# An attention kernel whose POOL engine takes over a quarter of the low parts, with value products carried over units

## The reference

```
x = x + tanh(g_xattn[i]) * attention_i(...)
x = x + tanh(g_ffn[i]) * experts_i(...)
```

```
dots = jnp.einsum('bhid,bhjd->bhij', q, k) * scale
attn = jax.nn.softmax(dots, axis=-1)
out = jnp.einsum('bhij,bhjd->bhid', attn, v)
return out @ Wo + bo
```

## Time and profile before

| | |
|---|---|
| median of 3 runs | 3818.83 us (3818.24 to 3830.18) |
| the profiled execution, its own time | 3806.05 us |
| its span, first to last instruction | 3804.4 us |
| PE busy | 3136.1 us (82%) |
| DVE busy | 1952.9 us (51%) |
| ACT busy | 1442.8 us (38%) |
| POOL busy | 698.3 us (18%) |
| granted clock of PE, mean | 0.864 of full speed |

### The profile page before, as it was taken

The page is one execution under the profiler, slowest core; times in us unless marked ns, Lnnn a source line. Parts: engine busy times, 40 slices in busy tenths (PEclk is TensorE's granted clock), DMA queues, the critical chain, the costliest instruction groups (busy, mean ns, idle before and its releaser), DMA issues. The chain is left out here.

```text
span 3804.4 us, 47742 instructions
## 1 busy us (share of the span) xinstructions
PE 3136.1 (82%) x13932; PEld 2131.8 (56%) x13933; DVE 1952.9 (51%) x3544; ACT 1442.8 (38%) x2976; POOL 698.3 (18%) x808
## 2 busy tenths in 40 slices
PE   7594769982898798999499999999999998349990
PEld 4493434432885477999356556555565664226650
DVE  3313454412453315444578777787777885613333
ACT  1131443430211113444346666666666666001100
POOL 0101021113103110000211112211112211061116
PEclk6697769995997568999689999999999999679995
DMA  1442000005232001000000000000000000324543
GB/s 34 151 146 70 1 1 1 1 1 197 87 103 62 13 0 45 23 22 1 9 6 2 8 1 7 5 4 6 2 7 1 7 1 3 136 99 152 167 141 109
DMA packets 136512, 174.12 MB, mean 46 GB/s; under 512 B 36345, under 2 KB 112784, under 8 KB 132784
## 3 DMA queue, kind: packets, MB, share of 16 engines
q1 hardware_dynamic: 104992, 103.23, 8.3%
q0 software_dynamic: 17072, 47.34, 3.8%
q10 hardware_dynamic: 14304, 22.02, 1.7%
HBM read 110.20 MB, written 62.00 MB: 45 GB/s over the span
## 5 line engine op out<-in xcount | busy, mean ns | idle before, releaser
L1853 DVE TENSOR_TENSOR l3a_pt_lo<-l3a_pt,l3a_pt_hi 128x512 fp32r<-128x512 f32 (+1 forms) x640 | 467.6, 733 | 161.3 <-ACT l3a_pt L1749 157.6
L1748 ACT ACTIVATE l3a_pt_hi<-l3a_banks 128x512 fp32r<-128x512 f32 (+1 forms) x640 | 381.8, 597 | 368.1 <-PE l3a_banks L1709 305.0
L1749 ACT ACTIVATE l3a_pt<-l3a_banks 128x512 f32<-128x512 f32 (+1 forms) x640 | 378.1, 591 | 0.0
L1828 DVE TENSOR_REDUCE l3a_maxima<-l3a_banks 128x1 f32<-128x1178 f32 x256 | 353.0, 1382 | 23.2 <-PE l3a_banks L1662 14.1
L1719 PE MATMUL l3a_banks<-l3a_q,l3a_k 128*128 128x512 f32 (+1 forms) x640 | 278.0, 434 | 26.2 <-ACT l3a_pt L1749 24.7
L1709 PE MATMUL l3a_banks<-l3a_pt_hi,l3a_v 128*65 128x512 f32 (+1 forms) x640 | 287.9, 450 | 2.0 <-ACT l3a_out L1762 1.6
L1720 PE MATMUL l3a_banks<-l3a_q,l3a_k 72*128 72x512 f32 (+3 forms) x640 | 256.9, 401 | 0.0
L1709 PE MATMUL l3a_banks<-l3a_pt_lo,l3a_v 128*65 128x512 f32 (+1 forms) x640 | 253.6, 396 | 0.0
L1709 PE MATMUL l3a_banks<-l3a_pt_hi,l3a_v_lo 128*65 128x512 f32 (+1 forms) x640 | 253.2, 396 | 0.0
L1662 PE MATMUL l3a_banks<-l3a_k,l3a_q 64*128 64x512 f32 (+1 forms) x768 | 210.8, 382 | 5.3 <-DVE l3a_maxima L1828 4.1
L1719 PEld LDWEIGHTS l3a_banks<-l3a_q,l3a_k 128*128 128x128 f32 (+1 forms) x640 | 117.3, 183 | 120.2 <-issue 37.8
(11 more groups left out here) (525 smaller groups left out, 6273.0 us busy)
## 6 DMA issues: line engine op xcount, KB each, us to landing
l3f_w<-in_L_ffn_w SPq DMA_DIRECT2D x96, 256.0 KB, 3.0
l0f_w<-in_L_ffn_W ACTq DMA_DIRECT2D x12, 1024.0 KB, 6.5
l3f_slots_x<-l3f_zeros SPq DMA_DIRECT2D x10, 1024.0 KB, 12.7
l1f_w<-in_L_ffn_W ACTq DMA_DIRECT2D x18, 512.0 KB, 4.6
l2f_w<-in_L_ffn_w SPq DMA_DIRECT2D x16, 512.0 KB, 4.3
l3f_x_rows<-l3f_slots_x SPq DMA_DIRECT2D x32, 256.0 KB, 4.1
l3f_slots_y<-l3f_y_rows POOLq DMA_DIRECT2D x32, 256.0 KB, 4.0
l1f_slots_x<-l1f_zeros SPq DMA_DIRECT2D x5, 1024.0 KB, 8.1
```

Of the source, the lines that this page charges most:

```text
L1748: act.activation(a.pt_hi[0:rows, n % a.pt_slots, :], a.st_bank[0:rows, n % 2, :], ACT.Exp, bias=bias, scale=scale)
L1749: act.activation(a.pt[0:rows, n % 4, :], a.st_bank[0:rows, n % 2, :], ACT.Exp, bias=bias, scale=scale).then_inc(a.exped, 1)
L1828: dve.tensor_reduce(a.maxima[:, n:n + 1], banks.rearrange("p a b -> p (a b)")[:, 0:KEYS], AX.X, ALU.max).then_inc(a.maxed, 1)
L1853: dve.tensor_tensor(a.pt_lo[0:rows, slot, :], a.pt[0:rows, n % 4, :], a.pt_hi[0:rows, slot, :].bitcast(F32), ALU.subtract).then_inc(a.lo_m ...
```

## The change

- Low parts: of every four slots of layer 3, the low part of the fourth (n = 3, 7, ..., 39) is made by POOL, in order with its other work; DVE makes the other three. PE and ACT wait for the one or the other engine's count (`low_of`). `pt_hi` and `pt_lo` have 5 buffers and not 6.
- POOL's program of a unit: before slot 14 it scales group 3 of the unit before, before slots 20, 30 and 39 groups 0, 1 and 2, and between them it makes the low parts in order of slots.
- The copies of q and k are DMAs on SP's queue, ahead of the totals of group 3 of the unit before; DVE inverts these totals in slot 12 and not in slot 4.
- The value products of a unit's last 4 (2) slots come in the first slots of the next unit, and so does the keeping of its group 3.
- The scores for the maxima are matmuls over 128 rows (rounded q twice against rounded k and the rest of k), and so wait for the copies of q and for all of k.
- In the last unit, four tiles of its own output projection run in slots 36 to 39, and four after it.
- The first unit stands before the loop: in layer 3 the loop has 6 rounds, 3 units follow it.

```
-        self.pt_slots = 6 if split else 4
+        self.pt_slots = 5 if split else 4
...
 def scores_pe(...)
+        project.keys_ready(pe, 0 if unit is None else unit, uses)
+        pe.wait_ge(a.q_doubled, 64 if unit is None else unit * 64 + 64)
-    lhs = a.q1[hi, u, h, t * P:(t + 1) * P]
+    lhs = a.q1[:, u, h, t * P:(t + 1) * P]
...
-        ins = pe.matmul(banks[:, c, 0:end - at], lhs, a.k1[hi, u, h, at:end], start=True, stop=not masked)
+        ins = pe.matmul(banks[:, c, 0:end - at], lhs, a.k1[:, u, h, at:end], start=True, stop=not masked)
...
 def attention_pe(...)
         if n >= a.lag:
-            multiply_values(n - a.lag)
-    for n in range(SLOTS_OF_UNIT - a.lag, SLOTS_OF_UNIT):
-        multiply_values(n)
+            multiply_values(unit, u, n - a.lag)
+        elif not is_first(unit):
+            multiply_values(unit - 1, 1 - u, SLOTS_OF_UNIT + n - a.lag)
...
 def attention_act(...)
+        if n == a.lag and not is_first(unit):
+            keep_group(act, a, unit - 1, GROUPS - 1)
...
-            act.wait_ge(a.lo_made, unit * SLOTS_OF_UNIT + (n + 1))
+            if not (is_first(unit) and n < a.exp_slots):
+                act.wait_ge(*low_of(a, unit, n - a.exp_slots))
...
 def attention_dve(...)
-        if a.split:
+        if a.split and not low_by_pool(a, n):
...
-def attention_pool(pool, a, unit, u, following=True):
-    scale_group(pool, a, number(unit, -1), 3, 1 - u)
+def attention_pool(pool, a, unit, u):
+    scaled_at = {14: -1, 20: 0, 30: 1, 39: 2}
+    for n in range(SLOTS_OF_UNIT):
+        if n in scaled_at:
+            g = scaled_at[n]
+            if a.split:
+                pool.wait_ge(a.lo_made_pool, unit * (SLOTS_OF_UNIT // 4) + n // 4)
+                pool.sem_inc(a.passed, 1)
+            scale_group(pool, a, number(unit, g), g % GROUPS, 1 - u if g < 0 else u)
+            pool.wait_ge(a.ot_done, number(unit, g) + 3)
+            pool.sem_inc(a.passed, 1)
+        if low_by_pool(a, n):
+            slot, rows = n % a.pt_slots, key_chunk(n % 10)[1]
+            pool.wait_ge(a.exped, unit * SLOTS_OF_UNIT + (n + 1 + 2))
+            pool.sem_inc(a.passed, 1)
+            pool.tensor_tensor(a.pt_lo[0:rows, slot, :], a.pt[0:rows, n % 4, :], a.pt_hi[0:rows, slot, :].bitcast(F32),
+                               ALU.subtract).then_inc(a.lo_made_pool, 1)
...
+def low_by_pool(a, n):
+    return a.split and n % 4 == 3
...
+def low_of(a, unit, n):
+    if low_by_pool(a, n):
+        return a.lo_made_pool, unit * (SLOTS_OF_UNIT // 4) + (n + 1) // 4
+    return a.lo_made, unit * (SLOTS_OF_UNIT // 4 * 3) + (n + 1 - (n + 1) // 4)
...
-def double_parts(pool, a, unit, u):
+def double_parts(sp, a, unit, u):
...
-                out, source = a.q1[other, u, h, columns], a.q1[hi, u, h, columns]
+                sp.dma_start(a.q1[other, u, h, columns].bitcast(F32), a.q1[hi, u, h, columns].bitcast(F32)).then_inc(a.q_doubled, 16)
```

More of the change, by code:

```diff
@@ L1615, in attention_prepare, with is_first @@
     pool.tensor_scalar(a.minus[:], chip.ident[0:8, 0:8], -1.0, None, ALU.mult).then_inc(a.prepared, 1)
+def is_first(unit):
+    return isinstance(unit, int) and unit == 0
 def number(unit, g):
@@ L1640, in side_pe @@
         ins = pe.matmul(bank[:, 0:D], a.out_t[:, 1 - u, t * P:(t + 1) * P], project.w_out(unit), start=True, stop=True)
+    elif name[0] == "e":
+        t = int(name[1])
+        if t % 4 == 0:
+            pe.wait_ge(a.ot_done, number(unit, 1 if t == 0 else 3) + 3)
+            project.w_out_ready(pe, unit + 1, 1 - u)
+        ins = pe.matmul(bank[:, 0:D], a.out_t[:, u, t * P:(t + 1) * P], project.w_out(unit + 1), start=True, stop=True)
     else:
@@ L1728, in attention_pe @@
                 if score_slot(m) == n:
[L1729 removed]
+                    scores_pe(pe, a, unit + 1, 1 - u, m, mask, uses, project)
         if n >= a.lag:
[L1731 to L1733 removed]
+            multiply_values(unit, u, n - a.lag)
+        elif not is_first(unit):
+            multiply_values(unit - 1, 1 - u, SLOTS_OF_UNIT + n - a.lag)
+    if not following:
+        for n in range(SLOTS_OF_UNIT - a.lag, SLOTS_OF_UNIT):
+            multiply_values(unit, u, n)
 def attention_act(act, a, unit, u, uses, scale, project, mask=None, following=True):
@@ L1755, in attention_act @@
                 project.act(act, unit + 1, 1 - u, n)
-    keep_group(act, a, unit, GROUPS - 1)
+    if not following:
+        keep_group(act, a, unit, GROUPS - 1)
 def keep_group(act, a, unit, g):
@@ L1965, in attention_units @@
 def attention_units(engine, pairs, cycle):
+    units = BATCH * pairs
+    cycle(0, 0, True)
     if pairs > 2:
[L1968 to L1975, removed]
+        with engine.Fori(0, pairs - 2) as i:
+            cycle(i * BATCH + 1, 1, True)
+            cycle(i * BATCH + 2, 0, True)
+    cycle(units - 3, 1, True)
+    cycle(units - 2, 0, True)
+    cycle(units - 1, 1, False)
 def add_bias_pool(pool, chip, xn_made, gb_made, gb):
@@ L2375, in extra @@
                         load_w_out(sp, pair)
-                    elif following_pair:
+                    elif not (isinstance(pair, int) and pair == PAIRS - 1):
                         sp.wait_ge(a.side_done, uses.done_with("v4"))
                         load_weights(sp, pair + 1)
[L2380 to L2386, removed]
+                attention_sync(sp, a, unit, u, following, extra)
+            double_parts(sp, a, 0, 0)
+            cycle(0, 0, True, 0)
+            with sp.Fori(0, PAIRS - 2) as i:
+                cycle(i * BATCH + 1, 1, True, None)
+                cycle(i * BATCH + 2, 0, True, i + 1)
+            cycle(BATCH * PAIRS - 3, 1, True, None)
+            cycle(BATCH * PAIRS - 2, 0, True, PAIRS - 1)
+            cycle(BATCH * PAIRS - 1, 1, False, None)
             attention_end(sp, None, None, a, BATCH * PAIRS - 1)
```

91 lines of the change are left out of this document (45 added, 46 removed).

## The result

The changed kernel takes 4248.99 us (median of 4 runs, 4228.48 to 4256.8), the kernel before 3818.53 us (4 runs, 3808.5 to 3830.18) beside it: a ratio of 1.112, with 1.107 to 1.117 as its interval. The prediction said 4211 us, 4100 to 4330. The profiled execution took 4250.62 us. The experiments ran on other chips, on which the kernel before takes 3784 to 3786 us, so they are compared by their ratios to it.

A forecast was written before the change was run, and what follows sets the result against it. PE was taken to set the end before the change, POOL's scaling to delay low parts after it: 3806.05 + 411 (layer 3) - 20 (layer 1) = 4197, times 1.0034 = 4211 us; range 4100 to 4330.

The forecast's parts named there:

- The price of POOL's scaling: POOL, each group: 6.2 us before the broadcast, 0.8 in it, 7.24 idle, 1.36 multiplying; 15.6 us, holding up what is queued.
- rival 1: Layer 3's low parts on POOL are not late; a unit is PE's 74 us; 3696 us as median; chance 0.05.
- rival 2: POOL's gap behind the broadcast goes, the one before it stays; scaling 8.4 us, unit 77; 3734 us as median; chance 0.03.
- The walk through a unit: Layer 3's steps between POOL's late low parts: 19.9 + 20.2 + 20.2 + 24.6 + 21.7 = 106.6 us against 81.35.
- The low part's own price: One 128x512 low part on POOL: 1.36 us taken, bounds 1.10 and 2.05, plus 0.35 for semaphores.
- The 4285 us: Whole kernel if POOL's seven low parts on the path each wait fully for DVE: 5 us a unit more.
- rival 3: PE's lower clock after stalls lasts twice the time seen: 3 to 5 us more a unit, 4270 to 4400; chance 0.12.
- Layer 1: Layer 1's attention gets 20 us shorter: 3 from carrying, 10 from 128-row maxima, 6 from a higher clock, rounded.
- carrying: Value products carried over units: nothing now in layer 3, where PE waits for low 39 anyway; some 3 us in layer 1.
- 128 rows: Maxima scores on PE: 72 us less work in layer 3, only lengthening most stalls; 10 us less in layer 1.
- The own output tiles at nothing: Four own output tiles in slots 36 to 39: 2 us of PE in each last unit, behind POOL, costing nothing.
- The copies: Doubling q and k by SP's DMAs: 0.5 us each to issue, landing in some 2.3 us; free, without cover up to 4 a unit.

The follow-up runs named there:

- row-by-DMA kernel: Changed kernel, low parts still on POOL, with the row of inverse totals spread over 64 partitions by DMA instead of POOL's broadcast: 0.9704, 3675.21 us.

## Why the prediction was right, and where it was off

**The price of POOL's scaling** (15.6 us a group, both gaps real): right. The row-by-DMA kernel takes away the broadcast alone and the waits go with it. Rivals 1 and 2 are out: the gap behind the broadcast is 7.3 us with low parts queued as without. The Trainium skill, GPSIMD Engine Reference, 2.1 Instruction dispatch, has a load of about 6 us at the first call to freshly loaded code, counted from MODIFY_POOL_CONFIG. The prediction took this as one load a group, and so as a case for rival 2. The trace agrees with the Trainium skill for the broadcast (6.0 us from the change), and it has a second change of code at the multiplication, 6.9 us ahead of it: two loads a group, if the return is one too, which is a reading and no run isolates it.

**The walk through a unit** held term by term: 20.2 measured 19.8, the next 20.2 was 20.1, 24.6 was 24.2, and 21.7 + 19.9 = 41.6 was 43.3 in unit 3 (over all units 20.1, 20.1, 24.5 and 42.5); the sum 106.6 was 107.25, the four waits of 5 to 9 us were 3.2 to 8.9. Over all units the waits for low 23 and low 31 are 3.0 to 5.4 us and not the 7 that 20.2 less 13 gives: PE's own part of a unit came to 83 us (1164.16 / 14) and not 74 and some 3 for the clock. The two middle waits are short and cost as much as the others: a step is set by POOL's chain, and what PE idles is only the rest, so PE's part could be this far off without showing in the time. The stage came to 421 us more where 411 was said. The 10 us lie in the stretch from low 39 to low 15: 8 in the 14 periods, 2 in the last unit.

**The low part's own price**: 1.36 taken, 1.31 measured on average over 160; the least is 1.25, the median 1.27, the longest 1.74. The 4285 us by the Trainium skill, SBUF — State Buffer, "Who interferes with whom", with every such meeting in full, are not borne out: few low parts can have met it, as the median shows.

**The clock** (rival 3) is the term that was too small. Put in were 3.5 us at the lower level behind low 39, from one loop start; measured were 4.6 to 7.7, on average 6.2 us, so rival 3's condition came true in some units. Of the steps from low 39 to low 15 those with 7.4 to 7.7 us at 0.50 take 43.0 to 43.3 us and those with 4.6 to 4.7 take 41.5 to 42.3, half a microsecond of time for each one more at half clock; 41.6 was said. It cost only about 1 us a unit, where rival 3 had 3 to 5, because this step alone goes by PE. Behind the other three waits the clock is low too, for 3 to 6 us, and POOL's chain covers it.

**Layer 1**: off. The term was -20, measured -3.3. Its first three units took 231.3 us instead of 239.8, so 8.5 of the 13 for carrying and maxima came; the 6 us for a higher clock in the first maxima did not (0.50 still, with 128 rows); and the last unit with its tail gave 5.2 back (96.8 for 91.6), with 23.2 us of PE's waiting in front of its own output tiles for POOL (20.0 before).

**The own output tiles at nothing**: right only because the waits for low parts cover them. Without these they hold PE for 11.0 us. All low parts on DVE gave 0.978 where rival 1, whose case it is, had 3696 us, 0.968: in that profile layer 1's attention is 14 us longer than rival 1 has it and layer 3's 22, of which 13 lie in the last unit with its tail and the rest in units of 75.1 us.

**The parts that gain** are there, as worked out: 128 rows 68 us by experiment (72 + 10 said), carrying about 23, DVE's busy time 129 us less (115 said). The copies are free by the trace: they land in 2.3 us and PE has no wait for one; no run undid them. SP's issue of one took 0.46 to 0.61 us, as reckoned (0.5):

```profile
l3a_q<-l3a_q SPq DMA_DIRECT2D x64, 128.0 KB, 2.3
L1988 SPq DMA_DIRECT2D l3a_k<-l3a_k x96: 461/533/606, 1913.1 to 3468.5; - x96
```

**Open**: the 27 us outside of the two attentions. They are not the change's: the run with two broadcasts has the whole change, and the same two stages take 1066.6 and 549.9 us there, 1066.8 and 550.1 in the kernel before, 1081.4 and 562.2 in this profiled execution. What made them longer there is not known. Of the 54 us between the 4197 worked out for a profiled execution and this one's 4250.62 they are half; the other half is in the parts that the prediction names, 418 us where it had 391.

## What to carry to other kernels

An engine with 20% of busy time may have no time to give: add up, from the timeline, what a step occupies from its first wait to the next instruction, the idle "issue" time too, and look at what is queued behind it. When work with a deadline is moved to such an engine, its place in the queue counts and not its share: ten low parts cost 506 us, and six, of which none is needed soon after a long step begins, cost 4 hundredths of the kernel's time instead of 13. Where a cross-partition copy on POOL switches its code, a DMA that spreads the row over partitions takes the long step out altogether (0.992 by itself, 0.9675 with the rest of the change).

## What was not expected of the hardware

- Two broadcasts in a row share the switch: 0.20 us between them, and the gaps of 6.4 and 7.2 us once around both.
- Layer 1's first maxima stayed at a granted clock of 0.50 for the 30 us shown, with 128 rows as with 64, though PE was busy 25.95 of 30 us.
- The clock stayed at 0.50 for longer after a wait than at the one loop start of the earlier trace rows: on average 6.2 us of full work after the waits for low 39, and the 9 us shown after one where the last products stood at the unit's end, instead of 3.5.
